# Third part of a split 3x3 convolution in four 64x64 tiles for both row halves at once, with an exchanged copy by DMA in place of the stacked one

## The reference, cut to what matters

```
x = x + window_attention(gn(x))            # 7x7 windows, 8 heads, cyclic shift by 3
x = x + binary_conv3x3(gn(x)) * box * alpha + bias
x = x + conv3x3(gn(x), sign(kernel2))      # the layer that the change is about
x = x + gated_block(gn(x))                 # 64->128, 4 taps along the tokens, silu gates, 128->64
```

## Time and profile before

| what | value |
|---|---|
| median of three executions | 218.71 us (217.41 to 220.54) |
| the profiled execution | 217.4 us |
| its span from first to last instruction | 215.5 us |
| busy PE, DVE, ACT, POOL | 203.2, 154.1, 138.9, 94.8 us |
| granted TensorE clock, mean of the span | 1.0 of full speed |

### The profile page before, as it was taken

How to read it: one execution, slowest core, us unless ns; L and a number is a source line. 1 busy time by engine, 2 the same in 40 slices (tenths; PEclk the granted TensorE clock), 3 DMA queues, 4 the chain that set the end, 5 groups by cost and what they waited for, 6 DMA issues and landing times.

```text
span 215.5 us, 6793 instructions
## 1 busy us (share of the span) xinstructions
PE 203.2 (94%) x2734; PEld 143.3 (66%) x2735; DVE 154.1 (71%) x316; ACT 138.9 (64%) x294; POOL 94.8 (44%) x108
## 2 busy tenths in 40 slices
PE   7788999999999999999999998997899999899994
PEld 2356888888888878888788865654566665445441
DVE  4665699977886868878769755999796862625543
ACT  2438598779776987788877762278444364876631
POOL 0349999970325199322792019487435200100000
PEclk9999999999999999999999999999999999999999
DMA  6970000000000000000000000001347700002032
GB/s 211 434 292 0 3 3 6 0 3 5 3 3 3 3 2 3 3 3 3 5 0 3 5 3 0 0 22 24 79 94 171 171 2 0 0 3 75 6 111 106
DMA packets 4701, 10.03 MB, mean 47 GB/s; under 512 B 704, under 2 KB 3520, under 8 KB 4544
## 3 DMA queue, kind: packets, MB, share of 16 engines
q1 hardware_dynamic: 4528, 9.27, 13.6%
q10 hardware_dynamic: 144, 0.34, 0.4%
HBM read 5.03 MB, written 1.61 MB: 31 GB/s over the span
## 4 chain that ended last, share of the span: by engine, by line
PE 75%; ACT 7%; DVE 6%; DMA 4%; POOL 3%; issue 3%; SPq 1%; ACTq 0%; POOLq 0%; DVEq 0%
PE turned L706 12%; PE outs L726 11%; PE scores L695 10%; PE scores L914 5%; PE scores L915 4%; PE qkv L666 4%; PE qkv L676 4%; PE scores L808 4%; PE turned L942 3%; PE scores L823 3%; PE outs L748 2%; PE turned L859 2%; DMA xw<-xw_in 2%; DMA p<-parts 2%; PE scores L932 2%
## 5 line engine op out<-in xcount | busy, mean ns | idle before, releaser
L1035 DVE TENSOR_REDUCE mx<-scores 113x16 f32<-113x784 f32 x32 | 30.9, 965 | 9.5 <-PE scores L695 9.3
L706 PE MATMUL turned<-cst,d 113*113 113x113 f32 x256 | 33.3, 273 | 0.9 <-DVE d L1040 0.9
L706 PEld LDWEIGHTS turned<-cst,d 113*113 113x113 f32 x256 | 27.8, 178 | 8.5 <-issue 7.1
L475 ACT ACTIVATE pt<-turned 113x392 f32<-113x392 f32 x64 | 28.4, 495 | 7.1 <-PE turned L706 5.8
L1040 DVE TENSOR_TENSOR d<-scores,mx 113x784 f32<-113x784 f32 x32 | 31.2, 976 | 1.1
L207 POOL TENSOR_TENSOR kex<-ks,cst 128x784 f32<-128x784 f32 (+1 forms) x16 | 23.2, 1452 | 18.6 <-ACT ks L454 18.5
L726 PEld LDWEIGHTS outs<-vsb,pt 113*49 113x49 f32 x1024 | 26.1, 125 | 6.1 <-issue 2.9
L287 POOL TENSOR_TENSOR rstd<-ve,mhalf 128x1 f32<-128x1 f32 (+1 forms) x15 | 8.7, 578 | 47.5 <-DVE ve L1001 47.3
L445 ACT ACTIVATE scores<-rel 113x784 f32<-113x784 f32 x32 | 26.2, 817 | 5.0 <-DMA rel<-rel_in 3.7
L726 PE MATMUL outs<-vsb,pt 113*49 113x18 f32 x1024 | 29.2, 199 | 0.0
L695 PE MATMUL scores<-kex,qs 32*49 32x196 f32 x512 | 28.2, 332 | 0.0
(11 more groups left out here) (121 smaller groups left out, 365.5 us busy)
## 6 DMA issues: line engine op xcount, KB each, us to landing
p<-parts SPq DMA_DIRECT2D x20, 112.5 KB, 2.3
x<-x_in SPq DMA_DIRECT2D x1, 1568.0 KB, 9.8
out<-res SPq DMA_DIRECT2D x8, 196.0 KB, 1.9
xw<-xw_in SPq DMA_DIRECT2D x2, 392.0 KB, 4.7
xw<-xw_in SPq DMA_DIRECT2D x1, 784.0 KB, 6.6
p<-parts SPq DMA_DIRECT2D x6, 108.8 KB, 2.8
ker<-ker_in SPq DMA_DIRECT2D x2, 288.0 KB, 10.1
late<-late_in SPq DMA_DIRECT2D x1, 417.0 KB, 10.7
```

The lines of the kernel that those rows point to most:

```text
L475: act.activation(pt[0:WK, k % 2, j].rearrange("p n (w t) -> p n w t", w=2), ps_t[j][0:WK, :].rearrange("p (n w t) -> p n w t", n=4, w=2)[: ...
L706: mm = pe.transpose(ps_t[j][0:WK, n * P:n * P + WK], d[0:WK, k % 2, h:h + 2, :].rearrange("p a b -> p (a b)")[:, 0:WK], ident[0:WK, 0:WK])
L1035: dve.tensor_reduce(top, sc, AXX, ALU.max).then_inc(max_done, 1)
```

## The change

The third part is now computed by `conv2_third(g)` for both halves at once. For each of the nine taps it issues four matmuls of 64 rows by 64 columns: half 0 of both images from `parts` on the partitions where the image lies, and half 1 of both images from `p3x`, in which each image's rows of part 2 for half 1 (16 rows) lie on the other image's partitions. So the four use the four quarters of the array, each bank is written by two of them (one from the upper and one from the lower rows of the array, into different partitions), and two of them with different data share each row half. Weights are `w2` alone. `p3x` comes from two DMAs for each g (0 too) of 64 x 960 bytes instead of four of 64 x 1,740 to 1,800 bytes. `conv_done` is raised by 2 at the end of both halves. PE waits for the copy also at g = 0, and SP waits for `p3_ready` of g = 0 before it issues the copies of g = 1. `w2b`, `w2z` and their five POOL instructions are gone. In the head, DVE masks the first keys before it takes the statistics of the second pair, and six fillers before `scores(0)` are two.

```diff
+        p3x = sb("p3x", [P, 2, HR + 2, PAD], BF16)
-                if g > 0:
-                    sp.wait_ge(p3_ready, g + 1)
-                    for row in range(2):
-                        for w in range(2):
-                            sp.dma_start(p33[64 * row:64 * row + 64, s, w, 0:PAD - row],
-                                         parts[64 * w:64 * w + 64, s, 2, row:PAD]).then_inc(thirds_stacked[s], 16)
+                sp.wait_ge(p3_ready, g + 1)
+                for w in range(2):
+                    sp.dma_start(p3x[64 * (1 - w):64 * (2 - w), s],
+                                 parts[64 * w:64 * w + 64, s, 2, HR:PAD]).then_inc(thirds_stacked[s], 16)
...
-                for ky in range(2):
-                    q = slice(64 * ky, 64 * ky + 64)
-                    pool.tensor_copy(w2b[q], w2[q, 3 * ky:3 * ky + 3]).then_inc(w2_ready, 1)
-                    pool.wait_ge(w2_ready, 3 + ky)
-                pool.memset(w2z[:], 0.0).then_inc(w2_ready, 1)
-                pool.wait_ge(w2_ready, 5)
-                for w in range(2):
-                    q = slice(64 * w, 64 * w + 64)
-                    pool.tensor_copy(w2z[q, w], w2[q]).then_inc(w2_ready, 1)
-                    pool.wait_ge(w2_ready, 6 + w)
...
-            filler(ps_t[1], 6)
+            filler(ps_t[1], 2)
...
-            def conv2_third(g, i):
-                if i == 0:
-                    pe.wait_ge(p3_ready, g + 1)
-                    if g > 0:
-                        pe.wait_ge(thirds_stacked[g % 2], 16 * 4 * ((g + 1) // 2))
...
+            def conv2_third(g):
+                pe.wait_ge(p3_ready, g + 1)
+                pe.wait_ge(thirds_stacked[g % 2], 32 * (g // 2 + 1))
+                for tap in range(NTAP):
+                    ky, kx = tap // 3, tap % 3
+                    for i in range(2):
+                        ps = bk[(2 * NG + 2 * g + i) % 4]
+                        for w in range(2):
+                            q = slice(64 * w, 64 * w + 64) if i == 0 else slice(64 * (1 - w), 64 * (2 - w))
+                            rhs = (parts[q, g % 2, 2, ky:ky + HR, kx:kx + HW] if i == 0 else
+                                   p3x[q, g % 2, ky:ky + HR, kx:kx + HW])
+                            mm = pe.matmul(ps[64 * w:64 * w + 64, 0:HALF], w2[q, tap], rhs,
+                                           start=False, stop=(tap == NTAP - 1))
+                mm.then_inc(conv_done, 2)
...
-            conv2_third(0, 0)
             conv2_stacked(0, 1)
-            conv2_third(0, 1)
+            conv2_third(0)
...
             dve.tensor_tensor(bt[:], ps_o[:, 0:1], ww("bp"), ALU.add).then_inc(bt_ready, 1)
+            dve.wait_ge(ks_ready, 1)
+            mask_keys(dve, 0, 0, 2).then_inc(kex_first, 1)
             dve.wait_ge(ld_x1, 16)
             window_moments(1).then_inc(gn_stats, 1)
-            dve.wait_ge(ks_ready, 1)
-            mask_keys(dve, 0, 0, 2).then_inc(kex_first, 1)
```

More of the change, by code:

```diff
@@ L130, in program @@
         p12 = sb("p12", [P, 2, 2, PAD, PAD], BF16)
-        p33 = sb("p33", [P, 2, 2, PAD, PAD], BF16)
-        w2b = sb("w2b", [P, 3, C], BF16)
-        w2z = sb("w2z", [P, 2, NTAP, C], BF16)
+        p3x = sb("p3x", [P, 2, HR + 2, PAD], BF16)
+        above = sb("above", [P, NTAP, C], BF16)
         xf = sb("xf", [P, 2, HW, HW])
@@ L346, in ternary_signs @@
                 pool.wait_ge(ld_k2, 16)
-                above = p33[:, 0, 0].rearrange("p a b -> p (a b)")[:, 0:NTAP * C].rearrange("p (t c) -> p t c", c=C)
-                pool.tensor_scalar(above, ker2[:], 0.0, None, ALU.is_gt)
+                pool.tensor_scalar(above[:], ker2[:], 0.0, None, ALU.is_gt)
                 pool.tensor_scalar(w2[:], ker2[:], 0.0, None, ALU.is_lt).then_inc(w2_ready, 1)
                 pool.wait_ge(w2_ready, 1)
-                pool.tensor_tensor(w2[:], above, w2[:], ALU.subtract).then_inc(w2_ready, 1)
+                pool.tensor_tensor(w2[:], above[:], w2[:], ALU.subtract).then_inc(w2_ready, 1)
                 pool.wait_ge(w2_ready, 2)
-                for ky in range(2):
-                    q = slice(64 * ky, 64 * ky + 64)
-                    pool.tensor_copy(w2b[q], w2[q, 3 * ky:3 * ky + 3]).then_inc(w2_ready, 1)
-                    pool.wait_ge(w2_ready, 3 + ky)
-                pool.memset(w2z[:], 0.0).then_inc(w2_ready, 1)
-                pool.wait_ge(w2_ready, 5)
-                for w in range(2):
-                    q = slice(64 * w, 64 * w + 64)
-                    pool.tensor_copy(w2z[q, w], w2[q]).then_inc(w2_ready, 1)
-                    pool.wait_ge(w2_ready, 6 + w)
             def border(t, value):
@@ L825, in conv2_stacked @@
                                   start=(tap == 0), stop=False)
-            def conv2_third(g, i):
-                if i == 0:
-                    pe.wait_ge(p3_ready, g + 1)
-                    if g > 0:
-                        pe.wait_ge(thirds_stacked[g % 2], 16 * 4 * ((g + 1) // 2))
-                ps = bk[(2 * NG + 2 * g + i) % 4]
-                if g > 0:
-                    for kx in range(3):
-                        for w in range(2):
[L837 to L845, removed]
+            def conv2_third(g):
[5 more added lines that the diff above has]
+                        ps = bk[(2 * NG + 2 * g + i) % 4]
+                        for w in range(2):
+                            q = slice(64 * w, 64 * w + 64) if i == 0 else slice(64 * (1 - w), 64 * (2 - w))
[4 more added lines that the diff above has]
+                mm.then_inc(conv_done, 2)
             def conv2(g):
@@ L849, in conv2 @@
                     conv2_stacked(g, i)
-                for i in range(2):
-                    conv2_third(g, i)
+                conv2_third(g)
             def channel_sums(g, i):
@@ L883, in _ @@
             conv1(3, 1)
-            pe.wait_ge(w2_ready, 7)
+            pe.wait_ge(w2_ready, 2)
             conv2_stacked(0, 0)
```

## The result

The changed kernel took 215.25 us (median of four, 214.94 to 215.54) against 218.75 us (217.41 to 220.54): a ratio of 0.987, 95% interval 0.984 to 0.991. Measured again beside its variants it gave 215.43 us (ratio 0.988, 0.985 to 0.991). The forecast was 215.4 us, and a change of less than 2%. The profiled execution has a span of 213.7 us, 1.8 less than before.

A forecast was written before the change was run, and what follows sets the result against it. PE was taken to bound the kernel (75% of the chain). Savings of 0.87, 0.41, 0.24 and 1.14 sum to 2.66 us: 214.7 from the profiled execution, 216.05 from the median; forecast between them, 215.4 us, range 213.3 to 218.3.

The forecast's parts named there:

- head, fillers: Before the first scores: four of PE's fillers fewer, 0.218 us each, start the scores earlier and shift the rest, -0.87 us.
- mask moved on DVE: Head: keys' mask moved ahead of the statistics only buys room; left in place it would still be 0.19 us ahead.
- pair 0, held by the statistics: Third layer, pair 0: of 1.4 us saved only 0.41 counts, since the next mix needs DVE's statistics, ending at 157.95.
- pair 1, wait for the third part's copy: Third layer, pair 1: PE's 0.24 us idle before the third part goes, as the second exchange DMA lands by 161.1.
- third part in four tiles, each pair: Third layer, pairs 1 to 3: nine rounds of 0.170 plus 0.13 give 1.66 us instead of 2.04, 0.38 less each.
- stacked copy of pair 3: Third layer: stacked copies were expected earlier with fewer issues on SP; no wait for them was in the sum.
- the signs that the prediction named: Third part 1.6 to 1.7 us, scores near 12.1, pair 0's mix near 157.2, gated block near 174.1, no "DMA p3x" idle.
- case E: Pairs 2 and 3: a copy or the statistics come late, up to 0.5 us each once, 215.2 to 215.7 us; chance 0.14.
- Rival B: Third part: tiles of different rows writing one bank take turns, 3.19 us instead of 2.04, total 219.8 us; chance 0.12.
- The failed step: Third layer: SP, with 14 issues of 0.6 us before, has 4 fewer for pairs 2 and 3, so stacked copies come earlier.
- (C): Head: with four fillers gone PE's clock could fall to 1.2 GHz, +2.4 us, total 217.1 us; chance 0.04.

The follow-up runs named there:

- the reordered halves: Changed kernel with each pair's 36 four-tile matmuls reordered, nine taps of half 0 first, then those of half 1: 218.10 us, ratio 0.998.
- variant with the mask behind: Changed kernel, still two fillers, but DVE masks the first keys after the second pair's statistics, as before the change: 216.67 us.

## Why the prediction was right

The time and the direction were right, and most steps were, but that the time was met so closely is luck in part (The level, below). Between the two profiled executions the gated block starts 1.89 us earlier (176.62 to 174.73 us), and the last matmul 1.88 earlier: what was gained there was kept to the end. By step:

| step | predicted | measured |
|---|---|---|
| head, fillers | 0.87 | 0.86 (0.70 with the later input) |
| mask moved on DVE | 0 | 0.1 |
| pair 0, held by the statistics | 0.41 | 0.43 |
| pair 1, wait for the third part's copy | 0.24 | 0.43 |
| third part in four tiles, each pair | 0.38 (1.66 us) | 0.38 (1.65 us) |
| stacked copy of pair 3 | 0 | -0.82 (-0.67 and -0.55 in two more profiles) |

Of the signs that the prediction named, the stretch of 1.65 us, the first scores at 12.18 and the mix behind pair 0 at 157.34 came true; the gated block came at 174.73 and not near 174.1, and PE's idle time was not where case E looked for it, but before the stacked matmuls of pair 3.

**The third part** was the central step. The price that I put together from column tiles that share rows and the scores' tiles that share columns, 9 x 0.170 + 0.13, came out at 1.65 us. The period of a pair fell from 5.75 (165.18 to 170.93) to 5.37. Rival B, turns in a bank, is refuted twice: by the starts at 161.1 and by the reordered halves, where pairs in one bank follow each other by 0.176 us. As a rule on time, the rule of the Trainium skill that it went by (TensorEngine Tiling (Array Packing), Gotcha 1: PSUM Pressure) does not hold for two row tiles that write different partitions of a bank.

**Pair 1's wait** was mis-sized. I took the 0.24 us that the profile writes on PE's idle time. It cost 0.43: pair 1 took 6.18 us from its stacked matmuls to those of pair 2 (159.00 to 165.18), where the period without a wait was 5.75. By the starts it is the same: the third part begins 3.49 us behind the stacked matmuls in pair 1 (159.00 to 162.49) and 3.08 in pair 2 (165.18 to 168.26). The idle time starts when the last modelled matmul ends, and that one's 0.33 us reach past the moment at which the next pair, 0.170 us behind, could have started.

**The failed step** is the sentence that SP "has 4 fewer for pairs 2 and 3, so the stacked copies come earlier". They did, by 2.3 us, the first at 163.61 instead of 165.87. But PE came to them 2.3 us earlier too, and the last landed in 3.9 instead of 2.3 us. I had used the longest landing that the trace showed, 3.5 us, for the exchange and not for the stacked copies. With it the last one (issued at 165.5) lands at 169.0, and PE wanted it at 168.6: a wait of 0.4 us. (The "14 issues" of that sentence are 16, four groups of four; nothing rests on it.) Case E had the mechanism, in the wrong transfer, and at up to 0.5 where it was 0.83.

**The level.** The forecast of 215.4 stood between the sum from the profiled execution, 214.7, and that from the median, 216.05. With the measured steps the sum is 2.04 instead of 2.66, and 217.5 less that is 215.5, which the executions at full clock bear out (215.3 to 215.4). The forecast hit because the half of the 1.3 us that I added for scatter about made up for the wait that I missed, which is luck. As a forecast of the mechanism it was 0.6 us too good. The change against the median, 3.3 us forecast and 3.5 measured, agrees by luck as well: the like-for-like change is 2.1 us, and the rest is the clock in the kernel before, for which the prediction's sum has no term.

**The clock in the head** (C) did not fall: in every profile the clock that is granted is the full one from the first scores until near 151 us at least.

## What to carry to other kernels

A tiled price that no row shows can be put together from rows that show each axis of it, and the cost of entering a tiling read from a stretch that does. When PE gets faster, give every transfer that it waits for the longest landing in the trace, not only the new ones, and count the DMAs that share its queue. And look for the idle stretch that drops the clock before comparing medians: here matmuls of zeros inside it cost nothing (217.30 us, against 217.3 at full clock beside it) and no execution fell to the levels 1.3 and 3.1 us above.

## What the runs showed of the hardware that I had not expected

- **Matmuls on free tiles run ahead of the program's order.** With half 0 before half 1, matmuls of half 1 started while six of half 0 had not. The starts are records of the profiler, and the chain bears them out: 2.53 us for the 36, where strict order would give 18 x 0.17 + 0.13, 3.2. The Trainium skill, TensorE: Matmul & The Clock Gate, Part 3: Packing small matmuls, states that matmuls are in strict order in start and end. The starts above speak against it for tiles that share no quarter of the array.
- **The clock falls behind a wait of 2.1 us, or it doesn't, in the same kernel.** The variant with the mask behind was caught in all its seven executions. In the five profiles of caught executions the half clock begins between 151.1 and 152.6 us, behind this wait. The windows of the variant with the mask behind (us, PE busy, PEld, DVE, ACT, POOL, granted clock, DMA share, GB/s):

```profile
148.90:151.20 2.30, 0.18 (x3) 0.04 (x1) 2.27 (x5) 0.91 (x1) 2.21 (x1) 1.00 0.11 27
151.20:154.60 3.40, 3.40 (x10) 2.17 (x12) 0.77 (x2) 1.74 (x3) 0.00 (x0) 0.54 0.36 86
```

PE did next to nothing in the first window; in the second it was at 1.2 GHz nearly all the time, ten matmuls where the changed kernel has 26. The changed kernel, with the same idle window (0.23 us busy), kept 2.4 GHz in its profile and in eight of ten executions (clocks of 1.0; of the other two, at 0.992, one took 216.68 us and the other 215.36, no longer than the rest). The kernel before was caught in 30 of the 52 executions that ran beside the variants. What decides it in an execution stays open; that the idle stretch is the place was tried: with eight matmuls of zeros in it, none of 30 executions of four kernels was caught.
